# Gather indices read from two whole tables on chip, in an unrolled POOL program, in place of an index ring

## The reference

```python
h = maximum(layernorm(x), 0.0)
# layer 0: a 64x64 weight for each of 16 edge types
msg = sum over r of (h[src] * (etypes == r)) @ weight[r]
x = x + segment_sum(msg, dst)
h = maximum(layernorm(x), 0.0)
# layer 1: an MLP over both ends and the edge's attributes
hid = relu(concat([h[src], h[dst], edge_attr]) @ W1 + b1)
x = x + segment_sum(hid @ W2 + b2, dst)
```

## Time and profile before

| | |
|---|---|
| median of 3 runs | 4649.59 us (4648.26 to 4660.03) |
| profiled execution | its span, first to last instruction: 5751.5 us; the page gives no other time of it |
| mean granted TensorE clock in it | 0.691 of full speed |
| busy | PE 2662.5, weight loads 2284.8, DVE 1342.3, ACT 718.8, POOL 3515.0 us |
| DMA | 239634 packets, 153.76 MB, mean 27 GB/s |
| gathers' queue | 106496 packets, 109.26 MB, 10.1% of the 16 engines |
| SP's queue | 130129 packets, 39.04 MB, 3.2% |

### The profile page before, as it was taken

How to read it: one execution, slowest core, us unless ns; L and a number is a source line. 1 busy time by engine, 2 the same in 40 slices (tenths; PEclk the granted TensorE clock), 3 DMA queues, 4 the chain that set the end, 5 groups by cost and what they waited for, 6 DMA issues and landing times.

```text
span 5751.5 us, 67195 instructions
## 1 busy us (share of the span) xinstructions
PE 2662.5 (46%) x21235; PEld 2284.8 (40%) x21235; DVE 1342.3 (23%) x2703; ACT 718.8 (12%) x1394; POOL 3515.0 (61%) x3343
## 2 busy tenths in 40 slices
PE   1444444444444444443345445554444445544545
PEld 1444443444344343343334434443433434433434
DVE  5322322333232232232311111111111111111111
ACT  2111110110110010010111111111111111111111
POOL 5776767677667667667455555555565555555554
PEclk9767766777676676676666666666667666666666
DMA  3111111111111111111111111111111111111111
GB/s 83 23 22 25 26 24 23 25 26 23 25 24 24 25 24 25 23 23 22 25 24 26 28 25 27 28 25 28 27 27 26 27 26 28 25 28 26 25 29 24
DMA packets 239634, 153.76 MB, mean 27 GB/s; under 512 B 177657, under 2 KB 177705, under 8 KB 239267
## 3 DMA queue, kind: packets, MB, share of 16 engines
q0 software_dynamic: 106496, 109.26, 10.1%
q1 hardware_dynamic: 130129, 39.04, 3.2%
q10 hardware_dynamic: 2642, 0.63, 0.1%
HBM read 133.39 MB, written 14.45 MB: 26 GB/s over the span
## 4 chain that ended last, share of the span: by engine, by line
another core or an unknown queue 55%; PE 21%; issue 14%; DVE 5%; ACT 3%; SPq 1%; DVEq 1%; POOL 0%; ACTq 0%; DMA 0%; POOLq 0%
PE ps L1146 6%; PE ps L1101 4%; PE ps L1094 3%; PE ps L1136 2%; PE ps L1128 2%; PE ps L1139 2%; ACT slots L773 1%; DVE onehot L1009 1%; SPq L513 1%; DVE slots L1023 1%; DVE acc L983 1%; ACT relus L807 1%; DVE onehot L922 1%; PE ps L1117 1%
## 5 line engine op out<-in xcount | busy, mean ns | idle before, releaser
L628 POOL DMA_INDIRECT rows<-p_table,idx x1664 | 1644.3, 988 | 1339.3 <-DMA idx<-in_src_dram 791.3
L628 POOL DMA_INDIRECT rows<-h_table,idx x1616 | 1816.4, 1124 | 835.6 <-issue 485.5
L1101 PE MATMUL ps<-slots,w_pairs 128*64 128x128 f32 x3328 | 632.2, 370 | 1082.7 <-ACT slots L773 855.9
L1101 PEld LDWEIGHTS ps<-slots,w_pairs 128*64 128x64 f32 x3328 | 563.5, 194 | 1142.6 <-issue 1036.9
L1146 PE MATMUL ps<-onehot,relus 128*65 128x128 f32 x3328 | 606.9, 358 | 832.8 <-ACT relus L807 485.9
L1146 PEld LDWEIGHTS ps<-onehot,relus 128*65 128x65 f32 x3328 | 555.4, 192 | 882.6 <-ACT relus L807 519.6
L1094 PE MATMUL ps<-onehot,rows 128*64 128x128 f32 x6656 | 593.3, 322 | 199.9 <-issue 178.7
L983 DVE TENSOR_TENSOR acc<-acc,ps 64x16 f32 x1664 | 271.8, 163 | 1563.4 <-PE ps L1101 830.3
L1094 PEld LDWEIGHTS ps<-onehot,rows 128*64 128x64 f32 x6656 | 516.6, 164 | 226.9 <-issue 199.9
L773 ACT COPY slots<-ps 128x512 f32<-128x512 f32 x416 | 238.1, 586 | 2046.8 <-remote 1504.1
L922 DVE TENSOR_TENSOR onehot<-key,iota_f 128x2048 f32<-128x2048 f32 x209 | 479.2, 2293 | 57.9 <-issue 33.5
(11 more groups left out here) (102 smaller groups left out, 720.9 us busy)
## 6 DMA issues: line engine op xcount, KB each, us to landing
rows<-p_table,idx POOLq DMA_INDIRECT x1664
rows<-h_table,idx POOLq DMA_INDIRECT x1616
q_win<-q_table SPq DMA_DIRECT2D x208, 48.0 KB
attr<-in_edge_attr_dram SPq DMA_DIRECT2D x209, 32.0 KB
q_table<-q SPq DMA_DIRECT2D x12, 360.0 KB
idx<-in_src_dram SPq DMA_DIRECT2D x208, 4.0 KB
idx<-src_tab SPq DMA_DIRECT2D x202, 4.0 KB
xs<-in_x_dram SPq DMA_DIRECT2D x6, 480.0 KB, 11.8
```

The costliest lines, as they stand in the source:

```text
L628: pool.indirect_dma_start(rows[:, u, t, :], None, table, bass.IndirectOffsetOnAxis(ap=idx[:, u, t:t + 1], axis=0)).then_inc(s, 16)
L1101: last = pe.matmul(node_ps[:, b, 0:T * W0], w_pairs[:, r, :], slots[:, b, :, r * W0:(r + 1) * W0], start=(r == 0), stop=(r == RP - 1))
```

## The change

A second table `src_tab1` holds the sources of all groups for layer 1. SP loads it from HBM in the prologue. POOL's gathers take their index column straight from `src_tab` (layer 0) and `src_tab1` (layer 1). `idx` serves only the first six groups. POOL waits itself for the consumers, by `slots_summed` in layer 0 and `pre_added` in layer 1, and its two loops are written out, 202 x 8 and 208 x 8 gathers. SP's index DMAs and their waits are gone; in layer 0 it only stores chunks (`all_chunks` runs `store_pq` for each chunk in a loop).

```diff
+        src_tab1 = sb("src_tab1", [P, G, T], i32)
...
@@ SP, after the two loads of base_row @@
+            sp.dma_start(src_tab1[:, 0:G - 1, :], src[0:(G - 1) * GE].rearrange("(g p j) -> p g j", p=P, j=T)).then_inc(tab1_in, 16)
+            sp.dma_start(src_tab1[:, G - 1, :], src[LAST:E].rearrange("(p j) -> p j", j=T)).then_inc(tab1_in, 16)
             for k in range(NA):
                 p, cols, rows_of = piece(k)
                 sp.wait_ge(h_made_a, k + 1)
...
@@ SP, layer 0 @@
             with sp.If(fits > 0):
-                sp.wait_ge(prep_copied, 4)
-                for u in range(EG, U):
-                    sp.dma_start(idx[:, u, :], src_tab[:, u, :]).then_inc(idx_in[u], 16)
-                def group(it, u):
-                    g = it * U + u
-                    wait_apart(sp, slots_summed, 2 * (g + 1))
-                    sp.dma_start(idx[:, u, :], src_tab[:, bass.ds(g, 1), :]).then_inc(idx_in[u], 16)
-                segments(sp, group, store_pq, at_end=True, begin=1)
-                sp.wait_ge(slots_summed, 2 * (AHEAD + G))
-                for u in range(U):
-                    sp.dma_start(idx[:, u, :], src[u * GE:(u + 1) * GE].rearrange("(p j) -> p j", j=T)).then_inc(idx_in[u], 16)
+                all_chunks(sp, store_pq)
...
@@ SP, layer 1, group @@
-                    if not first:
-                        begin = sp.value_load(start_row[0:1, bass.ds(g, 1)], min_val=0, max_val=LAST)
-                        wait_apart(sp, z_made, g + 1)
-                        sp.dma_start(idx[:, u, :], src[bass.ds(begin, GE)].rearrange("(p j) -> p j", j=T)).then_inc(idx_in[u], 16)
...
@@ POOL @@
-            def gather(table, u, t, s):
-                pool.indirect_dma_start(rows[:, u, t, :], None, table,
-                                        bass.IndirectOffsetOnAxis(ap=idx[:, u, t:t + 1], axis=0)).then_inc(s, 16)
+            def gather(table, u, t, at, s):
+                pool.indirect_dma_start(rows[:, u, t, :], None, table, bass.IndirectOffsetOnAxis(ap=at, axis=0)).then_inc(s, 16)
...
             with pool.If(fits > 0):
-                for u in range(EG, U):
-                    pool.wait_ge(idx_in[u], 16)
+                pool.wait_ge(prep_copied, 4)
+                for g in range(EG, G):
+                    if g >= U:
+                        pool.wait_ge(slots_summed, 2 * (AHEAD + g - U + 1))
                     for t in range(T):
-                        gather(h_table, u, t, rows_in[u])
-                with pool.Fori(1, NIT) as it:
-                    for u in range(U):
-                        wait_apart(pool, idx_in[u], 16 * (it + 1) if u >= EG else 16 * it)
-                        for t in range(T):
-                            gather(h_table, u, t, rows_in[u])
+                        gather(h_table, g % U, t, src_tab[:, g, t:t + 1], rows_in[g % U])
...
             pool.wait_ge(p_stored, 16 * (NC + 1))
             with pool.If(fits > 0):
-                with pool.Fori(0, NIT) as it:
-                    for u in range(U):
-                        wait_apart(pool, idx_in[u], 16 * (it + 1 + (NIT if u >= EG else NIT - 1)))
-                        for j in range(T):
-                            gather(p_table, u, j, rows_in[u])
+                pool.wait_ge(tab1_in, 32)
+                for g in range(G):
+                    if g >= U:
+                        pool.wait_ge(pre_added, AHEAD + g - U + 1)
+                    for j in range(T):
+                        gather(p_table, g % U, j, src_tab1[:, g, j:j + 1], rows_in[g % U])
```

More of the change, by code:

```diff
@@ L223, in gnn_kernel @@
         blocks_cleared = sem("blocks_cleared")
-        idx_in = [sem(f"idx_in_{u}") for u in range(U)]
+        tab1_in = sem("tab1_in")
         rows_in = [sem(f"rows_in_{u}") for u in range(U)]
@@ L641, in _ @@
                 for t in range(T):
-                    gather(x, u, t, rows_in[u])
+                    gather(x, u, t, idx[:, u, t:t + 1], rows_in[u])
             pool.wait_ge(flag_made, 1)
```

## The result

The kernel after took 4674.07 us (median of 10 runs, 4656.39 to 4686.67), the kernel before 4649.57 (10 runs): ratio 1.0051, 95% interval 1.0037 to 1.0065. That is slower by 24.5 us. But this holds for one kind of chip only. On three other chips, used in the later comparisons, the kernel before takes 5756 to 5860 us, and on one of them (C) the kernel after was timed again and has a ratio of 0.920. The profile that stands ahead of the prediction (span 5751.5) looks like those chips, the times beside it like the first; of which chips they were is not on record. So in this part a chip is named with each number: A (before 4647.3 us), B (5755.8), C (5860.1), D (5763.9). The comparison above is like A. Each of the four chips served in one comparison only, some minutes apart, so whether the difference belongs to the chip or to the time is not told apart; "chip" stands here for both.

A forecast was written before the change was run, and what follows sets the result against it. POOL's issue was taken to bound the timed kernel from end to end. Terms -1.8 - 1.5 + 20.7 + 0.4 = +17.8 took 4649.6 to 4667 us; own range 4660 to 4680, 8 in 10 within 4628 to 4725.

The forecast's parts named there:

- the sum from POOL's beat: Whole kernel: head, POOL's issue in both layers, hole and tail give a floor of 4639.9, or 4593 without consumer backlog.
- the cost of being profiled: Slow SP stretches behind 1141.4 us of index waits, taken as profiling only; span without these waits 4610, near the median.
- The floor's terms for the layers: POOL's gathers and issue gaps without index waits: 2301.9 us for layer 0, 2131.7 for layer 1.
- hole and tail: Between the layers 60.6 us and after the last gather 33; both said to contain a backlog of consumers.
- Items 1 and 2: Index DMAs and SP's waits go: -1.8 at the head, -1.5 at group 9; ring release by POOL's own waits: 0.
- Group 9's 1.5 us: Filling phase: group 9 waits 3.34 us for its index; direct release saves DMA and SP latency, about -1.5.
- A deeper ring wouldn't lift consumers that take 14.2 us a group: Layer 1 of the profiled execution, 2947/208 us a group: argument against a gain from the full ring of 8.
- item 2: Ring release: layer 1's index waited behind q_win, so 8 slots acted as 5; taken as 0, gain at most 57 us.
- Rival B: Layer 1 consumers over 41 us behind in places; full ring of 8 gains 45 us, at most 57: 4622; chance 0.19.
- Item 3: POOL's program written out, 3280 gathers in the layers: taken as 0, +41 us at the most for instruction supply.
- Item 4: SP's two src_tab1 loads at the head, on the path: +20.7 from base_row's rate, plus 0.4; bounds 13.1 and 95.7.
- rival F: POOL still waits, now on PE and DVE by name; time as the forecast; chance 0.40 together with it.

The follow-up runs named there:

- e2: Kernel before plus only the two loads of src_tab1, in the kernel after's place, result unused; chip A: 4663.7 us, ratio 1.0029.
- e0: Kernel before, unchanged, profiled once more on chip A: 4661.28 us, span 4659.5.
- e3: Kernel before with POOL's two loops written out, index ring kept; chip A: 4645.39 us, ratio 0.9995.
- e5: Kernel before, loops written out, layer 0 direct from src_tab, layer 1 with the ring, no second table; chip B: 5621.5 us, ratio 0.9772.
- e6: Kernel before, loops written out, layer 1 direct with the late second-table load, layer 0 with the ring; chip B: 5450.81 us, ratio 0.9455.
- e1: Kernel after with the src_tab1 loads moved behind the stores of h_table; chip A: 4659.27 us, ratio 1.0021 to the kernel before.

## Why the prediction was right, and where it was wrong

The forecast was 4667, slower; measured were 4674, slower, on a chip where POOL bounds the kernel from end to end. The main mechanism was right: the load of the second table stands on the path at the head (e2). That the sum came within 7 us is in part luck. It had 21.1 for the load, where e2 shows 13.5; it took off 3.3 for the start, where 1.2 were to be had; and it had nothing for the other 10 us, which no run explains. Several of its statements fail, and one of them matters more than the result.

- **What bounds the kernel.** "I take these for the cost of being profiled" is wrong as a reading of the 1141 us of index waits. Timed runs on chips B, C and D take that long (medians 5756, 5860, 5764), and on chip A even the profiled e0 has no such waits. So the sum from POOL's beat was right for the chip that the result came from, by way of a wrong reason: two numbers 24% apart were, by all that these runs show, of two chips, and I made one an artefact. On A the parts are head 111.3, layers 2336.9 and 2166.1, hole 29.4, tail 15.8. The floor's terms for the layers (2301.9 and 2131.7) were 35 us too low each; hole and tail (60.6 and 33) were 31 and 17 too high, and it was right to suspect a backlog in them.
- **Items 1 and 2.** The direct start brought 1.2 us at the head, not 1.8 (flag to first gather 1.78 in place of 2.94). Group 9's 1.5 us were not to be had: on A nobody waits there. Taking 0 for the release was right on A (unless it has a share in the 10 us left over), and badly off on the others: on C the direct layer 0 was worth 143 us and the direct layer 1 351. "A deeper ring wouldn't lift consumers that take 14.2 us a group" is the statement that failed there: with the index out of SP's queue, layer 1 fell from 2940 to 2592 us, 14.1 to 12.5 a group. The mechanism stood in item 2: the index is issued behind q_win, whose z is four groups back, so that eight slots act as five, as the rows of group 109 show. Where consumers are late by tens of us, five are too few. What makes the consumers late is not SP alone: PE is late too, and in the direct layer 1 it is PE that they wait for. Rival B, priced at 45 us gained and 57 at most, is the right one for layer 1 on those chips, with 351 us; for the 143 us of layer 0 it had no mechanism.
- **Item 3.** 0 was right (e3: 0.9995 on A; in e5 and e6 the written-out layer with the ring is as long as the looped one). By the Trainium skill's rule on branches ("Runtime: NRT & Kernel Launch", Instruction fetch mechanics) each turn of the loop would have been a cost if its target was not at hand; e3 shows none for POOL, and no row tells whether the target was at hand.
- **Item 4.** The place was right: on the path in full, gather at 125.96 (forecast 131), DVE's wait 36.5 (42). The size was too high: 15.1 us of hold and issue for 20.7 + 0.4, near the lower bound of 13.1. The row of base_row gave a rate per packet with its engines 85% busy; 14.69 us for 1656 pieces per engine are 8.9 ns each. The 10.5 ns per packet of the Trainium skill ("DMA: Bandwidth & Descriptors", Measured), 17.4 us as an estimate, was nearer than mine, and also too high; in e1 the same load held SP 16.47 us, 9.9 ns each.
- **What is left over.** The load explains 13.5 of some 24 us. The other 10 appear in the one variant on A that has the whole change but for the place of the load (e1, 1.0021) and have no place in the profiles: POOL has no waits in either, and layer 1 took 2152 (e3), 2166 (e0), 2171 (e2) with the ring against 2164 (after) and 2169 (e1) without. A candidate is how often a gather meets DVE's one-hot (below): what that adds over both layers is 377 us (e3), 381 (e0) and 391 (e2) with the ring, and 386 (e1) and 387 (after) without, which doesn't decide it. It was not isolated; the runs meant for it fell on chips B and C.
- **"The profile's span will again be long"** was wrong for the same reason as the first point: it was 4667.0. That its waits are "now named after PE and DVE" (and rival F) came true in the direct layers on chips B, C and D only; on a chip like A there were none.

## What to carry to other kernels

When profile and timed runs of one kernel are far apart, find out whether they are of the same chip before calling either an artefact, and price the change for both cases. A ring whose refill stands in an in-order queue behind other waits is shallower than its slots; giving the consumer's release straight to the engine that needs it saved 8% where the consumers were late, and where they were not, it came with 10 us (0.2%) that nobody has explained. Before placing a load, look at who is idle for it: behind the stores of h_table the same load no longer delayed the first gather, which came 16.0 us earlier. Edge lists loaded by 96 rows and the rest rather than by 103 or 104 brought that gather 34 us earlier, and the kernel 22 (5 to 40).

## What the runs showed of the hardware

- The same program took 4647 us on one chip and 5756 to 5860 on three others, at a mean granted clock of 0.756 to 0.776 and 0.686 to 0.700 (the runs of the kernel before on A, and on B, C and D), with SP's and DVE's register instructions late by up to 0.7 us each and PE's `pre_made` late by a median 5.1 us (e6). What makes them late is not shown, nor whether the lower clock is a cause or comes of PE's idle time; no run here tells the chip's memory from the recording of the instructions, which every run has.
- A gather that POOL starts under DVE's one-hot is longer. In the timeline of the kernel after:

```profile
1413.36 2.29 DVE L902 TENSOR_TENSOR onehot<-key,iota_f 128x2048 f32<-128x2048 f32 x1
...
1414.00 2.46 POOL L612 DMA_INDIRECT rows<-h_table,src_tab  x1 [0.30 <-issue]
```

  The gather takes 2.46 us in place of 0.94 and ends 0.81 after the one-hot. On A this adds 306 to 314 us to layer 0 (some 209 such gathers) and 63 to 80 to layer 1, 8% of the kernel. The Trainium skill ("SBUF — State Buffer", Who interferes with whom) says that a DVE instruction with two inputs in SBUF contends with a GpSimd instruction that reads SBUF; the gather, which reads its index column there, agrees. The same section reports a TENSOR_TENSOR as not stalling a DMA of POOL; this one does.
- Between the span and the execution's time lie 1.7 to 2.1 us in every run.
